# A pause of GpSimd at every twelfth gather of the edge records

## The chip, the cores and the metric

The kernel runs on one core of one Trainium2 chip, as a single launch. The metric is the device time of a run in microseconds (us); several runs are taken, and their median counts. Five engines work side by side, each on its own stream of instructions: TensorE (PE in the profile, its weight loads PEld), VectorE (DVE), ScalarE (ACT), GpSimd (POOL) and SyncE (SP). They meet only through semaphores. 16 DMA engines move data between HBM and SBUF. A gather, which fetches rows named by a list of indices, is issued by GpSimd.

## The reference

Four layers are computed over a graph of 3125 nodes (256 features) and 100000 edges. Each layer adds to `x` a graph part, a mixing part and then a feed-forward part:

```python
edge_index = jnp.stack([src, dst])
xn = _layernorm(x, axis=-1)
x = x + _L0_gnn_ref(xn, ..., src, dst) + _L0_mix_ref(xn[None], ...)[0]
x = x + _L0_ffn_ref(_layernorm(x, axis=-1)[None], ...)[0]
xn = _layernorm(x, axis=-1)
x = x + _L1_gnn_ref(xn, edge_index, edge_type_7, L1_gnn_weights) + _L1_mix_ref(xn[None], ...)[0]
...
```

The graph parts of layers 0, 2 and 3 sum over the edges that end in a node, and need for each edge its source node (`src`), its weight (`edge_weight`) and its attribute (`edge_weight1`). The graph part of layer 1 takes the edges by source and type.

## The kernel before, in words

**Order of the work.** The kernel is a chain of phases. In each phase every engine runs its own part, and a barrier of all engines ends it. First `store_records` writes one record of four numbers per edge (source, weight, attribute, 1) to HBM. `order_by_dst` sorts the edges by the node in which they end. Then `order_by_src` sorts them a second time, by source and type, for layer 1; its sort (`build_sort`) is a bitonic network on VectorE (L239 and L240 are one exchange), with 14 turns in which TensorE transposes the keys in eight pieces (L209) and ScalarE and VectorE take half of the result each (L224, L227, L267, L277). After the transposes of a turn TensorE signals once where the sort has gathers beside it, and twice where it has none.

**The gathers of the change.** Once the order by end node is known, the records have to be brought into it. `fetch_records` does that on GpSimd: 784 gathers, one for each column `k`, each of 128 records of 16 bytes, from `records` in HBM into `dst_order_record` in SBUF. Gather `k` belongs to lane `k % 8`, each lane has a semaphore, and a landed gather adds 16 to it. Before gather `k` is issued, the gather `k - 8` of the same lane must have landed. Nobody needs the records before `unpack_records`, so the gathers are spread in shares over phases in which GpSimd has no other work (`record_share`): 14 beside the making of the second sort's keys, 190 beside that sort, 30 beside `build_run_shares`, 6 beside the order of the chunks, 8 beside the splitting of keys, 18 beside `build_unit_tiles`, 14 beside the loads of `x`, and the other 504 beside the opening of layer 0 (`open0`, by `build_open`).

**The opening of layer 0.** Five groups of five tiles of 125 nodes. For each group VectorE normalizes (L1284 to L1300), TensorE transposes (L1252) and multiplies in pairs of units (L1497) into two pairs of PSUM banks, ScalarE copies each pair out (L1465), five pairs a group. VectorE then does the group's own steps (L1583 to L1603), and TensorE adds the products of keys and values (L1614). The copies go to one buffer `st`, so a group's copies wait until the steps and the products of the group before are done. A group therefore has seven results of TensorE that another engine waits for: the transposes, five pairs, the sum. L1552 is the first instruction of the phase after.

**Other gathers that are named below.** `build_sums` (L602 on GpSimd, L641 on TensorE) makes the two weighted sums of layers 1 and 2, with 880 gathers of 128 rows of 1 KB each; four gathers make a unit. `combine_pairs` (L3197 on GpSimd, L3207 on VectorE) has 50 gathers, and VectorE takes each as it lands.

Of the kernel before, what the change touches and what calls it, by code (L numbers as in the profile page):

```python
# [37 lines left out]
HOTS = 4  # L38
REC = 4
REC_LANES = 8  # L40
SHARES = (14, 190, 30, 6, 8, 18, 14)
EARLY = sum(SHARES)

# [504 lines left out]
def fetch_records(nc, pool, o, first, last):  # L548

    for k in range(first, last):  # L550
        lane, turn = k % REC_LANES, k // REC_LANES
        if turn:
            pool.wait_ge(o["fetched"][lane], 16 * turn)
        nc.gpsimd.indirect_dma_start(o["record"][:, k, :], None, o["records"], bass.IndirectOffsetOnAxis(ap=o["row"][:, k:k + 1], axis=0)  # L554
                                     ).then_inc(o["fetched"][lane], 16)


def record_share(nc, o, n):

    return lambda pool: fetch_records(nc, pool, o, sum(SHARES[:n]), sum(SHARES[:n + 1]))  # L560


def unpack_records(nc, c, o):

    with phase(nc, "unpack", "chain") as s, nc.Block() as block:
        @block.vector
        def _(dve):
            v = nc.vector
            own = Chain(dve, s["chain"])
            for lane in range(REC_LANES):  # L570
                dve.wait_ge(o["fetched"][lane], 16 * (CHUNKS_S // REC_LANES))
            for b in range(TILES - 1):
# [2360 lines left out]
def layer0(nc, c, m, I, dram, by_dst):  # L2933

    with nc.sbuf_tensor("gnn0_to_dst", [R, TILES, D], F32) as to_dst:
        m["to_dst"] = to_dst
        open0(nc, c, m, I, dram, lambda pool: fetch_records(nc, pool, by_dst, EARLY, CHUNKS_S))
        unpack_records(nc, c, by_dst)
        with nc.sbuf_tensor("gnn0_acc", [R, TILES, D + 4], F32) as acc:
            build_attend0(nc, c, by_dst, dram["el0"], to_dst, I["L0_gnn_attn"], acc, dram["pairs"])  # L2940

            def keep(v, own, act_step):

                own(v.tensor_copy(m["deg3"][:], acc[:, :, D + 1:].rearrange("p t k -> p k t")))
            bulk(nc, "degrees", keep)
            close0(nc, c, m, I, acc)
# [352 lines left out]
def build(nc, I, out):  # L3299
# [8 lines left out]
    with ExitStack() as ctx:  # L3308
# [3 lines left out]
        by_dst["record"] = ctx.enter_context(nc.sbuf_tensor("dst_order_record", [P, COLS_S, REC], F32))  # L3312
        by_dst["fetched"] = [nc.alloc_semaphore(f"records_in{l}") for l in range(REC_LANES)]
        by_dst["records"] = dram["records"]
# [37 lines left out]
```

## Time and profile before

| what | value |
|---|---|
| timed runs, median of 3 | 9703.57 us (9694.26 to 9703.69) |
| profiled execution, span from first to last instruction | 10401.4 us |
| profiled execution, time outside the span | none is recorded |
| GpSimd busy in the profiled execution | 4458.2 us (43%) |
| TensorE busy | 6311.5 us (61%) |
| VectorE busy | 4856.6 us (47%) |
| ScalarE busy | 2031.2 us (20%) |

The profile comes from one execution that was recorded by the hardware profiler, and the median from runs that were not recorded. Here the recorded execution is the longer one, by 10401.4 - 9703.6 = 697.8 us. Busy shares are means over stages with different limits, so the stretches and the timeline say more than the shares. In the rows, a time in square brackets is how long the engine had stood idle, and behind the arrow is what ended that idle time; "issue" means that the profile shows nothing that it waited for, and "remote" that the wait was for another engine's signal that can't be tied to one instruction.

### The profile page before, as it was taken

Reading aid. Unit: us, or ns where it says so; the run is one execution under the profiler, and the core shown is the slowest. Engines: PE = TensorE matmul, PEld = TensorE weight load, DVE = VectorE, ACT = ScalarE, POOL = GpSimd, SP = SyncE. Lnnn points to the kernel's source line nnn. Section 1 sums busy time; section 2 is a strip of 40 time slices with the busy share of each in tenths; the row PEclk is TensorE's granted clock in tenths of the full one; section 3 lists DMA queues with packets and bytes.
Section 4 is the critical chain, followed back from the end, with each engine's and each line's share of the span. In section 5 each row is a group of like instructions: output and inputs, shape, how many; then the busy total and the mean of one; then the engine's idle time right before and its main releaser. Section 6 shows DMA issues by size and latency. Waiting matters only on the chain. (4 is left out here: it accounts for less than half of the span.)

```text
span 10401.4 us, 95746 instructions
## 1 busy us (share of the span) xinstructions
PE 6311.5 (61%) x28050; PEld 4795.7 (46%) x28050; DVE 4856.6 (47%) x13537; ACT 2031.2 (20%) x5038; POOL 4458.2 (43%) x4412
## 2 busy tenths in 40 slices
PE   0001115999996865454665444453965788887699
PEld 0000004888884433333443333342863676776466
DVE  7561216888884532222242222264113566666633
ACT  0000002444443210000120000012212232232322
POOL 0546772666660036666104666602020566664000
PEclk9998557999997986666676666675987777777799
DMA  0001002333330133333102333301960232222000
GB/s 12 6 1 28 7 4 71 83 83 83 83 83 14 46 108 92 94 92 92 35 11 70 94 92 92 92 18 25 316 221 27 77 81 80 80 81 64 11 13 19
DMA packets 404431, 697.45 MB, mean 67 GB/s; under 512 B 154143, under 2 KB 267784, under 8 KB 403421
## 3 DMA queue, kind: packets, MB, share of 16 engines
q0 software_dynamic: 206848, 480.68, 17.1%
q1 hardware_dynamic: 197076, 210.68, 6.3%
q8 instruction: 236, 3.87, 0.2%
q14 instruction: 271, 2.22, 0.1%
HBM read 631.46 MB, written 59.47 MB: 66 GB/s over the span
## 5 line engine op out<-in xcount | busy, mean ns | idle before, releaser
L658 POOL DMA_INDIRECT att_rows<-el_table,dst_order_row x1520 | 1589.4, 1046 | 1067.4 <-issue 387.0
L641 PE MATMUL sum_sum<-sum_rows,sum_hot 128*125 128x256 f32 x3520 | 1227.5, 487 | 1291.4 <-issue 817.1
L641 PEld LDWEIGHTS sum_sum<-sum_rows,sum_hot 128*125 128x125 f32 x3520 | 824.8, 240 | 1694.4 <-issue 1540.9
L602 POOL DMA_INDIRECT sum_rows<-rel_table,src_order_row x880 | 833.0, 947 | 1042.3 <-ACTq L593 629.2
L602 POOL DMA_INDIRECT sum_rows<-el_table,dst_order_row x880 | 833.0, 947 | 956.7 <-ACTq L593 543.7
L554 POOL DMA_INDIRECT dst_order_record<-records,dst_order_row x784 | 813.7, 1038 | 589.2 <-PEq L458 297.1
L624 DVE TENSOR_TENSOR gnn_acc<-gnn_acc,sum_sum 125x256 f32 x440 | 180.6, 410 | 1888.8 <-DMA ffn1e_w<-in_L_ffn_W_dram 938.7
L1136 PE MATMUL att_sum<-att_rows,att_hot 128*125 128x265 f32 x1280 | 429.3, 492 | 36.4 <-ACT att_part L1203 30.5
L800 PE MATMUL att_found<-gnn_to_dst,att_hot_t 125*128 x1760 | 437.8, 392 | 2.5 <-ACT att_hot_t L849 1.8
L658 POOL DMA_INDIRECT dst_order_record<-el_table,dst_order_row x240 | 266.1, 1109 | 400.4 <-SPq L960 240.5
L824 PE MATMUL att_sum<-att_rows,att_hot 128*125 128x261 f32 x1760 | 427.3, 385 | 2.4 <-ACT att_rows L862 2.4
L862 ACT ACTIVATE att_rows<-att_rows,att_p 128x257 f32<-128x257 f32 x880 | 375.8, 498 | 0.0
L1101 PEld LDWEIGHTS att_found<-layer_a_dst,att_hot_t 125*128 125x128 f32 x1760 | 275.9, 227 | 180.6 <-issue 159.4
L1136 PEld LDWEIGHTS att_sum<-att_rows,att_hot 128*125 128x125 f32 x1280 | 293.4, 241 | 114.7 <-issue 46.9
L1101 PE MATMUL att_found<-layer_a_dst,att_hot_t 125*128 x1760 | 254.4, 268 | 140.1 <-issue 84.2
L800 PEld LDWEIGHTS att_found<-gnn_to_dst,att_hot_t 125*128 125x128 f32 x1760 | 319.7, 192 | 38.0 <-issue 3.1
L824 PEld LDWEIGHTS att_sum<-att_rows,att_hot 128*125 128x125 f32 x1760 | 314.2, 188 | 47.8 <-ACT att_rows L862 2.5
L744 DVE CUSTOM_DVE_ANT_0 att_high<-att_high,att_att 128x256 f32<-128x256 f32 x880 | 320.0, 418 | 0.0
L1162 ACT COPY att_hot_t<-att_turn_p 125x512 f32<-125x512 f32 x220 | 129.1, 587 | 802.7 <-PE att_turn_p L1091 461.7
L809 PE MATMUL att_spread_p<-ident,att_score 128*125 128x128 f32 x1760 | 251.6, 286 | 43.2 <-issue 27.2
L739 DVE TENSOR_TENSOR att_high<-att_rows,att_found 128x1024 f32<-128x1024 f32 x220 | 268.7, 1222 | 6.5 <-issue 6.5
L809 PEld LDWEIGHTS att_spread_p<-ident,att_score 128*125 128x125 f32 x1760 | 210.0, 188 | 130.6 <-issue 85.1
(775 smaller groups left out, 12593.2 us busy)
## 6 DMA issues: line engine op xcount, KB each, us to landing
block_w<-in_L_ffn_W_dram SPq DMA_DIRECT2D x112, 512.0 KB, 6.3
block_w<-in_L_ffn_W_dram SPq DMA_DIRECT2D x56, 1024.0 KB
att_rows<-el_table,dst_order_row POOLq DMA_INDIRECT x1520
rel_table<-open_st SPq DMA_DIRECT2D x25, 784.0 KB
sum_rows<-rel_table,src_order_row POOLq DMA_INDIRECT x880
sum_rows<-el_table,dst_order_row POOLq DMA_INDIRECT x880
dst_order_record<-records,dst_order_row POOLq DMA_INDIRECT x784
pairs<-zeros SPq DMA_DIRECT2D x1, 7168.0 KB
```

The lines of the kernel that those rows point to most:

```text
L554: nc.gpsimd.indirect_dma_start(o["record"][:, k, :], None, o["records"], bass.IndirectOffsetOnAxis(ap=o["row"][:, k:k + 1], axis=0)).then_ ...
L602: nc.gpsimd.indirect_dma_start(rows[l][:, g, :], None, table, bass.IndirectOffsetOnAxis(ap=o["row"][:, k:k + 1], axis=0)).then_inc(s[f"row ...
L641: last = nc.tensor.matmul(slot(u), hot[u % HOTS_S][:, g, :], rows[l][:, g, :], start=(g == 0), stop=(g == G - 1))
L658: nc.gpsimd.indirect_dma_start(rows[l][:, g, 0:width], None, table, bass.IndirectOffsetOnAxis(ap=o["row"][:, k:k + 1], axis=0)).then_inc(s ...
L739: v.tensor_tensor(high[:], rows[u % LANES_A][:, :, 0:D], found[:], ALU.max).then_inc(s["picked"], 1)
L744: last = v.tensor_tensor_reduce(high[:, g, :], high[:, g, :], att[:], 0.8, 0.0, ALU.mult, ALU.add, score[u % 2][:, g:g + 1])
L800: last = t.matmul(found[:, g, :], hot_t[u % TURNED][:, g * P:(g + 1) * P], nodes_of_unit(to_dst, tile), start=True, stop=True)
L809: last = t.matmul(spread_p[:, g * P:(g + 1) * P], score[u % 2][:, g:g + 1].to_broadcast([P, R]), c["ident"][:], start=True, stop=True)
L824: last = t.matmul(sums[u % 2][:, 0:S], hot[u % HOTS][:, g, :], rows[u % LANES_A][:, g, :], start=(g == 0), stop=(g == G - 1))
L862: last = a.activation(own_rows[:, g, 0:D + 1], own_rows[:, g, 0:D + 1], ACT.Copy, scale=p[u % 2][:, g:g + 1])
L1101: done = t.matmul(found[u % 2][:, g, 0:H], hot_t[u % 2][:, g * P:(g + 1) * P], nodes_of_unit(to_dst, tile), start=True, stop=True)
L1136: done = t.matmul(sums[u % SUMS_B][:, 0:W + 1], hot[u % HOTS_B][:, g, :], rows[u % LANES_B][:, g, :], start=(g == 0), stop=(g == G - 1))
```

## The change

Ahead of a gather whose number within its share is 12, 24, 36 and so on, GpSimd waits until the gather that it issued last has landed. The number of gathers, their order, their lanes and their shares stay as they are.

```diff
@@ -38,6 +38,7 @@
 HOTS = 4
 REC = 4
 REC_LANES = 8
+REST_R = 12
 SHARES = (14, 190, 30, 6, 8, 18, 14)
 EARLY = sum(SHARES)
 
@@ -551,6 +552,8 @@
         lane, turn = k % REC_LANES, k // REC_LANES
         if turn:
             pool.wait_ge(o["fetched"][lane], 16 * turn)
+        if k > first and (k - first) % REST_R == 0:
+            pool.wait_ge(o["fetched"][(k - 1) % REC_LANES], 16 * ((k - 1) // REC_LANES + 1))
         nc.gpsimd.indirect_dma_start(o["record"][:, k, :], None, o["records"], bass.IndirectOffsetOnAxis(ap=o["row"][:, k:k + 1], axis=0)
                                      ).then_inc(o["fetched"][lane], 16)
```

## Rows read from the trace of the kernel before

**Rows 1.** The page: span, and the gathers' group (busy us, mean ns, idle before).

```profile
span 10401.4 us, 95746 instructions
...
L554 POOL DMA_INDIRECT dst_order_record<-records,dst_order_row x784 | 813.7, 1038 | 589.2 <-PEq L458 297.1
```

**Rows 2.** Busy time by stretch: both sorts, the opening with and without gathers.

```profile
44.00:292.00 248.00, 27.57 (x112) 21.97 (x112) 212.72 (x338) 10.02 (x22) 0.00 (x0) 1.00 0.00 0
355.00:706.00 351.00, 27.57 (x112) 21.97 (x112) 213.22 (x338) 8.74 (x21) 191.86 (x190) 1.00 0.03 1
...
914.00:1543.00 629.00, 111.90 (x250) 57.52 (x250) 120.37 (x139) 35.41 (x38) 486.33 (x466) 0.59 0.06 5
1543.00:1676.00 133.00, 43.05 (x108) 23.06 (x108) 65.61 (x37) 10.56 (x12) 0.00 (x0) 0.63 0.04 10
```

**Rows 3.** Timeline of GpSimd: ends of the first share, of the sort's, of the opening's.

```profile
351.35 0.94 POOL L554 DMA_INDIRECT dst_order_record<-records,dst_order_row  x1 [0.30 <-issue]
355.54 1.39 POOL L554 DMA_INDIRECT dst_order_record<-records,dst_order_row  x1 [3.24 <-SPq L202]
...
604.05 0.94 POOL L554 DMA_INDIRECT dst_order_record<-records,dst_order_row  x1 [0.30 <-issue]
...
1541.88 0.94 POOL L554 DMA_INDIRECT dst_order_record<-records,dst_order_row  x1 [0.30 <-issue]
```

**Rows 4.** Timelines of GpSimd, TensorE and VectorE where gathered rows are waited for.

```profile
3763.59 0.95 POOL L602 DMA_INDIRECT sum_rows<-rel_table,src_order_row  x1 [0.30 <-issue]
...
3766.46 3.75 PE L641 MATMUL sum_sum<-sum_rows,sum_hot 128*125 128x256 f32 x8 [0.55 <-DMA sum_rows<-rel_table,src_order_row]
...
7802.18 1.20 POOL L3197 DMA_INDIRECT combine_rows<-results,ffn_place  x1 [0.30 <-DVE X L3207]
...
7806.32 0.48 DVE L3207 SCALAR_TENSOR_TENSOR X<-combine_rows,ffn_gates,X 125x256 f32<-125x256 f32 x1 [0.90 <-DMA combine_rows<-results,ffn_place]
```

**Rows 5.** Timelines of TensorE and ScalarE in the opening, under the gathers.

```profile
985.14 3.55 PE L1497 MATMUL open_unit<-open_w_el,open_xT 128*125 128x512 f32 x4 [16.18 <-ACT open_st L1465]
988.53 1.88 PE L1497 MATMUL open_unit<-open_w_kv,open_xT 128*125 128x512 f32 x4
...
984.08 1.01 ACT L1465 COPY open_st<-open_unit 125x1024 f32<-125x1024 f32 x1 [21.39 <-remote]
1006.48 1.01 ACT L1465 COPY open_st<-open_unit 125x1024 f32<-125x1024 f32 x1 [21.39 <-remote]
1028.88 1.01 ACT L1465 COPY open_st<-open_unit 125x1024 f32<-125x1024 f32 x1 [21.39 <-remote]
```

**Rows 6.** Timeline of VectorE in the opening: starts of a group's work, the stage's end.

```profile
1030.02 1.49 DVE L1583 TENSOR_TENSOR open_row<-open_st,open_bias 125x1280 f32<-125x1280 f32 x1 [104.04 <-ACT open_st L1465]
...
1235.97 1.49 DVE L1583 TENSOR_TENSOR open_row<-open_st,open_bias 125x1280 f32<-125x1280 f32 x1 [139.24 <-issue]
...
1578.60 1.49 DVE L1583 TENSOR_TENSOR open_row<-open_st,open_bias 125x1280 f32<-125x1280 f32 x1 [67.15 <-ACT open_st L1465]
...
1635.22 1.49 DVE L1583 TENSOR_TENSOR open_row<-open_st,open_bias 125x1280 f32<-125x1280 f32 x1 [23.03 <-ACT open_st L1465]
...
1675.71 0.61 DVE L1552 SCALAR_TENSOR_TENSOR KV<-open_kv_p,block 128x128 f32<-128x128 f32 x2 [6.91 <-PEq L86]
```

**Rows 7.** The two sorts by tile: first and last start of the exchanges' first line.

```profile
L239 DVE TENSOR_TENSOR dst_order_keys<-dst_order_keys x153: 691/692/694, 44.9 to 290.4; 128x512 f32<-128x512 f32 x153
...
L239 DVE TENSOR_TENSOR src_order_keys<-src_order_keys x153: 691/692/746, 355.4 to 704.3; 128x512 f32<-128x512 f32 x153
```

**Rows 8.** Timelines of GpSimd and VectorE where the short shares end.

```profile
750.49 1.65 POOL L554 DMA_INDIRECT dst_order_record<-records,dst_order_row  x1 [0.30 <-issue]
...
752.05 6.55 DVE L395 RECIPROCAL src_order_keys<-runs_new 128x1024 f32<-128x1024 f32 x1
...
354.95 0.43 DVE L251 TENSOR_SCALAR src_order_keys<-src_order_keys 128x512 f32<-128x512 f32 x1 [6.19 <-PEq L86]
```

**Rows 9.** The gathers of the two weighted sums: first and last start.

```profile
L602 POOL DMA_INDIRECT sum_rows<-rel_table,src_order_row x880: 940/946/1027, 3754.8 to 4999.8; - x176
```

## The prediction, made before the change was run

> **What bounds the kernel now.** I read the page first, for the gathers' own group, and there the reader is to see that `fetch_records` is a stream of 784 instructions on GpSimd of 1038 ns each, with a small gap between them [rows 1]. Then I cut the busy time by stretch, to see in which stages that stream is the longest thing. In the opening of layer 0 GpSimd works from 914 to 1543 us through 466 gathers, while VectorE has 120 us of work and TensorE 112; in the 133 us that follow there are no gathers at all and the stage still runs [rows 2]. The third look is the timeline of that stage. TensorE ends a pair of units at 988.53 + 1.88 = 990.4 us, and ScalarE copies a pair at 1006.48 and the next at 1028.88, always 22.40 us after the one before [rows 5]. A group of five tiles takes 1235.97 - 1030.02 = 206 us under the gathers and 1635.22 - 1578.60 = 56.6 us once they are over [rows 6]. So something under the gathers delays what TensorE hands on. The two sorts say the same: identical work spans 290.4 - 44.9 = 245.5 us without gathers and 704.3 - 355.4 = 348.9 with 190 of them, 103.4 us more [rows 7].
>
> **Whether those delays are in the timed runs** is what this prediction hangs on. The profiled span is 10401.4 us [rows 1], the timed median 9703.6: 697.8 us of the span are not there without the recording. What would the delays add up to if they were all of the recording's making? 103 in the sort [rows 7]; 133 in the opening, whose work of five groups at 56.6 us (283) fits inside the gathers' 629 [rows 2, 6]; and in the two weighted sums, whose 880 gathers start over 4999.8 - 3754.8 = 1245 us [rows 9] where 879 steps of 0.95 + 0.30 [rows 4] need 1099, 146 each. Together 103 + 133 + 292 = 528 of the 698. No other 500 us that recording could have added is visible to me, so I take it as likelier than not that in the timed runs handed-on results are prompt, and GpSimd's stream alone sets the end of both stages. The Trainium skill, "NOTIFIC — the notification-queue block", section 7.1, says that the block's internal pipeline always holds its producers back rather than lose a record; by that rule the delays belong to the recording. Its section 10 says that a record costs an engine nothing at the rates it measured, which speaks against. No trace of this kind can show the unrecorded run.
>
> **The change part by part.** Nothing is removed or moved. One wait is added ahead of gather k when k - first is 12, 24, ...: in shares of 14, 190, 30, 6, 8, 18, 14 and the last of 784 - 280 = 504 that is 1, 15, 2, 0, 0, 1, 1 and 41, in all 61. It wants all 16 counts of gather k - 1, so it cannot pass before those rows have landed. Queued behind it on GpSimd are only the share's other gathers; who waits for these is the barrier that ends each phase, and last `unpack_records`. The eight-lane wait already there passes more easily after a pause.
>
> *Price of one wait.* No gather of this line is waited for at once in the trace, so I bound it. The fourth gather of a unit in the sums ends at 3763.59 + 0.95 = 3764.54 and TensorE, released by it, starts at 3766.46: 1.92 us. The last gather of the combination ends at 7802.18 + 1.20 = 7803.38 and VectorE takes it at 7806.32: 2.94 [rows 4]; both engines stood idle before, so it was the landing that they waited for. From these the usual gap of 0.30 comes off: 1.62 to 2.64 us. Nothing below 1.62 is likely: these are the quickest landings, and the wait cannot end earlier than the landing. The sums' gathers have the same duration (0.94 to 0.95) as the records' [rows 3, 4], so I stay near that row, but the first gather after a pause took 1.39 instead of 0.94 [rows 3]; I take 1.9. The Trainium skill, "DMA: Bandwidth & Descriptors", section on the anatomy of a DMA of the GpSimd path, gives about 2.0 us fixed for a whole DMA, plus bytes by rate. Counted from the instruction's start that would leave 2.0 - 0.94 - 0.30 = 0.8 us for a wait, an estimate, and by it the sum below would be 46 us and not 109; the landings in the trace (2.87 us from start) disagree, and I go by them.
>
> *The opening, 41 waits.* GpSimd ends at 1542.8 and in the prompt case all else has 629 - 283 = 346 us of room. Nothing hides the waits: 41 x 1.9 = 77.9 us. (If VectorE's work were as long as the stream, they would cost nothing.)
>
> *The sort, 15 waits.* The share runs from 355.54 to 604.99 [rows 3]; the prompt sort, begun at 354.95 [rows 8], would end some 245.5 + 1.4 later, at 602. GpSimd is level with it already, so 15 x 1.9 = 28.5 us. If the stream without recording runs at 1.25 us a gather, it ends at 593 and 9 us of that are covered.
>
> *The short shares.* The first share's last gather ends at 352.29 and the sort's first instruction comes at 354.95 [rows 3, 8]: GpSimd is last there, 1.9 us. In the runs' share the gathers end at 752.14 and VectorE's reciprocal only at 758.60 [rows 8]: 2 x 1.9 = 3.8 are hidden by 6.5 (without that cover, 3.8). The unit tiles' share I cost at nothing, as VectorE's copies close that phase; the one beside the loads of x at half, 1.
>
> Sum: 77.9 + 28.5 + 1.9 + 1.0 = 109.3 us. Within the profiled execution this is added to a prompt version of the span, since its own span contains the disputed 528; against the median, 9703.6 + 109.3 = 9813. With the low price 41 x 1.62 + 15 x 1.62 - 9 = 82, so 9785; with the high one 58 x 2.64 = 153, so 9857.
>
> **The rivals.**
>
> *A, faster: the delays are real and a pause lets everything waiting pass.* For it: while GpSimd stands still nothing is delayed (the last group, 56.6 us). A cycle becomes 12 x 1.25 + 1.9 = 16.9 us. Two pairs of units would pass in one pause, so a group has some five delayed hand-offs instead of seven: 5 x 16.9 + 36 of VectorE's work = 120 us. The opening's work, 5.4 groups (629/206 + 133/56.6), then needs 650 us and fits inside the stream; the stage ends with it at 1621 + 3 instead of 1676, -52. The sort's 103 us of delay would fall to some 68 (eight waits of half a cycle), -35. With 3 us of the short shares: -84, 9620. Against it: the 698 us need another source, and a pause of 2 us is short beside delays of 22. It decides if the opening loses more than 78 of its 133 trailing microseconds.
>
> *B, no change: the delays are real and each pause lets one result pass.* The 22.4 us become 16.9: a group takes 206 - 7 x 5.5 = 167.5 us, by 1621 us 4.2 of 5.4 groups are done and 1.2 x 56.6 = 67 us trail: +12. The sort gains 16, the short shares cost 3. About 9703.
>
> *C, slower by less: the delays are real and the pauses do not touch them.* The stream ends 78 us later, in which 78/206 of a group is done that would have taken 21 us afterwards: +57. The sort, where half of the 28.5 us are under work that goes on anyway, +12; short shares +3. About 9775.
>
> *D, the change does nothing:* if landings came before the next gather is dispatched, every wait would pass at once. The 1.92 us after the instruction's end speak against it; I count it in B.
>
> **How the numbers follow.** My forecast (prompt hand-offs, GpSimd sets the end, 61 waits) has 0.67; A 0.13; B with D 0.13; C 0.07. A measurement tells about 0.2%, 19 us. Slower: forecast and C, 0.74; within 0.2%: 0.13; faster: 0.13. The forecast's own range is 9785 to 9857. To leave out no more than 2 in 10 the range must take in C and B and may leave out A and the outer tails: 9680 to 9862.
>
> **What would show it.** In the changed kernel the gathers' line must wait for its own DMA 61 times more than the 5 of before, near 2.2 us each, 0.3 of it taken from the gaps called issue. The timeline must show such a pause after every twelfth gather and nowhere else. If the recording makes the delays, the span need not grow by 109: it may even shrink where pauses relieve the recording, while the timed median grows; span and median going apart would be the strongest sign for my reading. The step of ScalarE's copies in the opening tells A (several at once), B (about 17 us) and C (22.4). The prediction is wrong if the timed runs have the delays too, or if VectorE's part of the sort is longer than GpSimd's when nothing is recorded, which takes off up to 28.

## The result, and the profile after

| kernel | median, us | runs | span of the profiled run |
|---|---|---|---|
| before | 9698.9 (9688.7 to 9703.7) | 4 | 10401.4 in the first profile, 9692.3 in the second |
| changed | 9814.8 (9811.6 to 9820.4) | 4 | 9810.3 |

The ratio is 1.0125, with a 95% interval from 1.0111 to 1.0140: 116 us slower. Forecast were 9813 and a range from 9680 to 9862.

One thing of the section on the profile before has to be put right here. The recorded execution of the changed kernel is itself one of its four timed runs (9812.4 us, span 9810.3), and so it is in every experiment below; the three first timed runs of the kernel before have no span on record, but all 44 later ones have, 2.1 to 2.2 us under their times. So the later profiles show timed runs, and "recorded" and "timed" are no longer two kinds of execution.

The gathers' line of the changed kernel, by source. It answers to the group in [rows 1]; the list under it says what ended GpSimd's idle time before these gathers, in us, and how often:

```profile
L557 POOL DMA_INDIRECT dst_order_record<-records,dst_order_row x784: 938/944/4736, 334.5 to 1580.4; - x196
...
  issue: 219.8, 715
  DMA dst_order_record<-records,dst_order_row: 162.3, 62
...
DMA to landing us min/median/max: 2.2/2.3/13.8
```

The waits for the own DMA are there: 62 of them, 162.3 us. 61 are the added ones and one is a lane wait, where before has 4 or 5 of these: the pauses have let the others land. The last line gives the time from issue to landing, 2.3 us in the median. The timeline of GpSimd in the opening shows one of the pauses: 2.06 us of idle where 0.30 stands otherwise, twelve gathers after it the next.

```profile
925.82 0.94 POOL L557 DMA_INDIRECT dst_order_record<-records,dst_order_row  x1 [0.30 <-issue]
928.83 0.94 POOL L557 DMA_INDIRECT dst_order_record<-records,dst_order_row  x1 [2.06 <-DMA dst_order_record<-records,dst_order_row]
930.08 0.94 POOL L557 DMA_INDIRECT dst_order_record<-records,dst_order_row  x1 [0.30 <-issue]
...
942.55 0.94 POOL L557 DMA_INDIRECT dst_order_record<-records,dst_order_row  x1 [0.30 <-issue]
945.59 1.92 POOL L557 DMA_INDIRECT dst_order_record<-records,dst_order_row  x1 [2.10 <-DMA dst_order_record<-records,dst_order_row]
```

The span needs care. The profile of the changed kernel is 591 us shorter than the first one of before, while its timed runs are 116 us longer. ScalarE's copies in the opening, which stood 22.40 us apart in [rows 5], are now 3.4 us apart, though the gathers run beside them as before:

```profile
928.78 1.01 ACT L1468 COPY open_st<-open_unit 125x1024 f32<-125x1024 f32 x1 [2.12 <-PE open_unit L1500]
932.13 1.01 ACT L1468 COPY open_st<-open_unit 125x1024 f32<-125x1024 f32 x1 [2.34 <-PE open_unit L1500]
935.57 1.01 ACT L1468 COPY open_st<-open_unit 125x1024 f32<-125x1024 f32 x1 [2.42 <-PE open_unit L1500]
```

So the first profile can't be what the changed kernel is compared with. The first experiment was to take it again.

### The profile page after: what moved, and what is told of

Read it like the earlier page. It is cut to its first block and busy times, and to the rows that moved or that the text cites. A ratio compares the mean times of both kernels' runs of the same rounds, so it can differ in the third digit from the quotient of the medians.

```text
span 9810.3 us, 95807 instructions
## 1 busy us (share of the span) xinstructions
PE 6260.3 (64%) x28050; PEld 4792.7 (49%) x28050; DVE 4858.7 (50%) x13537; ACT 2039.4 (21%) x5038; POOL 4480.7 (46%) x4412
## 5 line engine op out<-in xcount | busy, mean ns | idle before, releaser
L644 PE MATMUL sum_sum<-sum_rows,sum_hot 128*125 128x256 f32 x3520 | 1262.5, 521 | 961.7 <-DMA sum_rows<-rel_table,src_order_row 467.9
L644 PEld LDWEIGHTS sum_sum<-sum_rows,sum_hot 128*125 128x125 f32 x3520 | 863.7, 257 | 1360.5 <-issue 1020.9
L793 PE MATMUL att_turn_p<-ident,att_hot 128*125 128x128 f32 x880 | 155.1, 299 | 468.6 <-DVE att_hot L671 457.6
L793 PEld LDWEIGHTS att_turn_p<-ident,att_hot 128*125 128x125 f32 x880 | 113.5, 188 | 510.4 <-DVE att_hot L671 510.2
L3200 POOL DMA_INDIRECT combine_rows<-results,ffn_place x50 | 61.7, 1233 | 466.6 <-PEq L3194 451.7
```

Of the source, the lines that this page charges most:

```text
L644: last = nc.tensor.matmul(slot(u), hot[u % HOTS_S][:, g, :], rows[l][:, g, :], start=(g == 0), stop=(g == G - 1))
L793: last = t.transpose(turn_p[:, g * P:(g + 1) * P], hot[u % HOTS][:, g, :], c["ident"][:])
```

## The experiments

**The kernel before, profiled again.** No edit.

> The kernel before, unchanged, profiled once more, to see whether the long span of its first profile (10401.4 us beside a median near 9700) belongs to every recording or to that one execution. If every recording delays what TensorE hands on (what my prediction supposed): a span near 10400 again, ScalarE's copies in the opening 22.4 us apart, the second sort 103 us longer than the first. If the delays belonged to that one execution: a span near 9700, copies some 3.4 us apart, the two sorts equally long, and the opening ending with its last gather near 1500. If the delays are in the timed runs too (the rivals), the time itself would have to hold them, and a span near 9700 can't show them.

One run of 9694.4 us, its span 9692.3. The delays are gone: the copies come 3.36 us apart, and the second sort, which spanned 348.9 us in [rows 7], spans 245.9.

```profile
899.54 1.01 ACT L1465 COPY open_st<-open_unit 125x1024 f32<-125x1024 f32 x1 [2.57 <-PE open_unit L1497]
902.90 1.01 ACT L1465 COPY open_st<-open_unit 125x1024 f32<-125x1024 f32 x1 [2.35 <-PE open_unit L1497]
```

```profile
L239 DVE TENSOR_TENSOR src_order_keys<-src_order_keys x153: 691/692/748, 355.5 to 601.4; 128x512 f32<-128x512 f32 x153
...
L602 POOL DMA_INDIRECT sum_rows<-rel_table,src_order_row x880: 942/946/1070, 3541.1 to 4643.7; - x176
```

The gathers of the first sum, from first to last start, take 4643.7 - 3541.1 = 1102.6 us, where they took 1245 in [rows 9]; 879 steps of 1.25 had been reckoned at 1099. All three places that I had added up to 528 us were prompt. And this is a recorded execution, so recording alone doesn't make the delays: they belonged to the one execution of the first profile. Two more executions were recorded to see whether they come back.

> The kernel before, unchanged, a third recorded execution, to see whether the delayed hand-offs of the first profile come back. If they come with a share of the executions: a span near 10400 with some chance. If they were rare: near 9690, as in the second profile.

> The same once more: near 10400 if the delays come often, near 9690 if they are rare.

They ran 9697.2 and 9699.9 us, with spans of 9695.1 and 9697.8. The delays did not come again.

With the second profile of before there is a fair partner. Busy time of each engine in two parts of its opening (us; PE, PEld, DVE, ACT, POOL, granted clock, DMA share, GB/s):

```profile
755.00:1130.00 375.00, 122.14 (x343) 66.49 (x344) 185.84 (x175) 46.76 (x51) 287.39 (x236) 0.76 0.10 15
1130.00:1466.00 336.00, 3.76 (x17) 3.25 (x16) 0.00 (x0) 0.00 (x0) 252.96 (x269) 0.51 0.05 3
```

In the last 336 us GpSimd issues 269 gathers and VectorE and ScalarE do nothing at all: the stage waits for GpSimd alone. In the sort it is the last as well, by some 6 us (the last exchange of VectorE and the last gather of the share):

```profile
601.96 0.68 DVE L240 TENSOR_TENSOR src_order_keys<-src_order_keys 128x512 f32<-128x512 f32 x1
...
607.52 0.94 POOL L554 DMA_INDIRECT dst_order_record<-records,dst_order_row  x1 [0.30 <-issue]
```

Then a ledger of where the 116 us arise, from the places where one phase hands over to the next. Of before, second profile:

```profile
355.03 0.43 DVE L251 TENSOR_SCALAR src_order_keys<-src_order_keys 128x512 f32<-128x512 f32 x1 [6.23 <-PEq L86]
...
616.08 0.98 POOL L330 IOTA runs_place<- 128x1024 int32 x1 [7.62 <-ACTq L327]
...
670.13 0.94 POOL L554 DMA_INDIRECT dst_order_record<-records,dst_order_row  x1 [5.99 <-ACTq L290]
...
732.82 0.94 POOL L554 DMA_INDIRECT dst_order_record<-records,dst_order_row  x1 [13.55 <-PEq L2112]
...
755.06 0.94 POOL L554 DMA_INDIRECT dst_order_record<-records,dst_order_row  x1 [5.08 <-POOLq L86]
...
1463.69 0.94 POOL L554 DMA_INDIRECT dst_order_record<-records,dst_order_row  x1 [0.30 <-issue]
...
1472.05 0.61 DVE L1552 SCALAR_TENSOR_TENSOR KV<-open_kv_p,block 128x128 f32<-128x128 f32 x2 [344.00 <-PEq L86]
```

Of the changed kernel:

```profile
357.02 0.43 DVE L252 TENSOR_SCALAR src_order_keys<-src_order_keys 128x512 f32<-128x512 f32 x1 [7.96 <-PEq L87]
...
644.31 0.98 POOL L331 IOTA runs_place<- 128x1024 int32 x1 [7.62 <-ACTq L328]
...
698.71 0.94 POOL L557 DMA_INDIRECT dst_order_record<-records,dst_order_row  x1 [3.97 <-ACTq L291]
...
761.37 0.94 POOL L557 DMA_INDIRECT dst_order_record<-records,dst_order_row  x1 [11.73 <-PEq L2115]
...
787.08 0.94 POOL L557 DMA_INDIRECT dst_order_record<-records,dst_order_row  x1 [3.45 <-POOLq L87]
...
1580.36 0.94 POOL L557 DMA_INDIRECT dst_order_record<-records,dst_order_row  x1 [0.30 <-issue]
...
1588.71 0.62 DVE L1555 SCALAR_TENSOR_TENSOR KV<-open_kv_p,block 128x128 f32<-128x128 f32 x2 [431.80 <-PEq L87]
```

A share's entry in the last column is how late the changed kernel is where the next phase takes over, less how late it was one line above.

| share | waits | forecast, us | later at its end, us |
|---|---|---|---|
| keys, 14 | 1 | 1.9 | 357.02 - 355.03 = 2.0 |
| sort, 190 | 15 | 28.5 | 28.2 - 2.0 = 26.2 |
| runs, 30 | 2 | 0 | 28.58 - 28.23 = 0.4 |
| chunks, parts, tiles | 1 | 0 | 28.55 - 28.58 = 0.0 |
| loads of x, 14 | 1 | 1.0 | 32.0 - 28.5 = 3.5 |
| opening, 504 | 41 | 77.9 | 116.7 - 32.0 = 84.7 |
| sum | 61 | 109.3 | 116.7 |

Behind the opening both kernels run alike: at its end the changed one is 1588.71 - 1472.05 = 116.7 us late, and at the end of the span 9810.3 - 9692.3 = 118.0.

**The opening's waits alone, and the sort's alone.** In the two kernels the condition reads

```diff
+        if first >= EARLY and k > first and (k - first) % REST_R == 0:
```

and

```diff
+        if first == SHARES[0] and k > first and (k - first) % REST_R == 0:
```

> Only the 41 waits of the opening's share. If GpSimd's stream sets that stage's end: in the profile of the changed kernel a wait stands as 2.06 us of idle instead of 0.30, so 41 x 1.76 = 72 us slower (60 to 90), 0.6 to 0.9%. If all 61 waits cost the same wherever they stand (rival): 41/61 of 116 = 78 us, which this run alone does not tell apart; together with the next run it does. If delayed hand-offs were real in timed runs and pauses relieved them: less than 40 us, or faster.

> Only the 15 waits of the share beside the sort. If GpSimd is level with VectorE there, as I predicted: 15 x 1.76 = 26 us slower, 0.27%. If VectorE's sort is the longer one when nothing is delayed: less, down to nothing. If a pause also makes the rest of the stream slower: more than 26.

The opening's waits: 9790.1 against 9706.6 us, ratio 1.0084 (1.0071 to 1.0098), 82 us. The sort's: 9727.7, ratio 1.0023 (1.0013 to 1.0033), 22 us. 82 + 22 = 104 of 116; the 5.5 us that the ledger gives the first share and the loads of x are in neither, and the other 6 or 7 are within the intervals. The opening has two thirds of the waits and the sort a quarter, so the uniform price of 1.9 us (116/61) would ask for 78 and 29: within their intervals this pair does not refute it. The ledger does, in which three waits beside the runs and tiles cost 0.4 us together. The expectation above had hoped that the two runs together would tell the rival apart; they don't.

**Twice as many waits in the opening.**

```diff
+        if first >= EARLY and k > first and (k - first) % (REST_R // 2) == 0:
```

> Waits in the opening's share alone, but at every sixth gather: 504 / 6 - 1 = 83 instead of 41. If each wait costs its landing less the usual gap (2.07 - 0.30 = 1.77 us) and the stage is GpSimd's throughout: 83 x 1.77 = 147 us, and with the larger price of the first few, which stand under the loads of the weights, up to 165; 1.5 to 1.7%. If the price comes from something that happens once or is bound to the total time (a rival): near the 0.84% of the 41 waits. If pauses let other work pass more quickly: less than twice the 41 waits' price.

9839.2 against 9695.0 us, ratio 1.0149 (1.0134 to 1.0165): 144 us for 83 waits, 1.74 each. 41 cost 82, so the price is paid per wait, and the work of the other engines gains nothing by the pauses. In its trace the waits of the opening read

```profile
POOL dst_order_record L557 <- DMA dst_order_record<-records,dst_order_row: 198.1, 82, 14.5
```

That is more idle time than 144 us ask for, even less the usual gaps (82 x 0.30) and less the 17.1 us of lane waits that before has; another saving hides in the 1.74. The 504 gathers themselves are busy for 521.8 us there, 18.5 less than the 540.4 of the second profile of before. Gathers of 1.8 to 3.5 us, instead of 0.94, are found while VectorE does a group's own steps of up to 2.8 us; before has 35 of them in the opening, this kernel 24. That fewer gathers meet those steps when there are more pauses fits this, but no run was made to show it.

**The same places, but a landing that is already past.**

```diff
+            pool.wait_ge(o["fetched"][(k - 4) % REC_LANES], 16 * ((k - 4) // REC_LANES + 1))
```

> The same 61 places, but the wait is for the gather four back, which was issued some 5 us before and by the landing of 2.2 to 2.3 us from issue has landed. If the price of the change is the landing: same time as before, within 10 us. If it is the wait instruction itself or the break in the stream: slower by tens of microseconds, up to the 116 of the change.

9710.2 against 9706.6 us, ratio 1.0005 (0.9996 to 1.0014): no difference, or at most 14 us, 0.2 a wait. The waiting list of GpSimd in this kernel (us in total, times, longest) shows why:

```profile
POOL dst_order_record L557 <- issue: 222.1, 728, 0.6
POOL dst_order_record L557 <- DMA dst_order_record<-records,dst_order_row: 36.8, 49, 8.4
```

49 idle times are put down to a DMA, but most are the usual gap of 0.3 us, and with the lane waits that before has as well they sum to 36.8 us. Only under the loads had the fourth gather back not landed: the added wait beside the loads of `x` took 3.71 us and one of the first in the opening 4.57. The instruction and the break in the stream cost nothing that can be measured; the landing is the price.

**More results of TensorE under the gathers.** The opening's call loses its pairing:

```diff
-    ... hand=(ACT.Sqrt,), pool_work=pool_work, st_lanes=1, pair=True)
+    ... hand=(ACT.Sqrt,), pool_work=pool_work, st_lanes=1)
```

> The kernel before with the opening's units handed over one by one: ten results of TensorE a group to be copied by ScalarE instead of five pairs, so 25 more hand-offs under the gathers, and no waits added. If hand-offs are prompt in timed runs: they are under GpSimd's stream, which ends some 340 us after the stage's other work, so same time within 10 us. If each result of TensorE needed 22.4 us there, as in the first profile: 25 x 22.4 = 560 us slower, less what follows the last gather.

9696.9 against 9695.0 us, ratio 1.0001 (0.9992 to 1.0010). The edit does add the hand-offs: ScalarE's copies of this kind number 200 instead of 175. With delays of 22.4 us they would have shown, since the stage then trails the gathers ([rows 2]) and nothing covers them. In the timed runs TensorE's results are prompt.

**Eight gathers moved to where GpSimd stood still.**

```diff
-SHARES = (14, 190, 30, 6, 8, 18, 14)
+SHARES = (14, 190, 30, 6, 8, 26, 14)
```

> The kernel before with 8 gathers moved from the opening's share to the one beside the unit tiles (26 instead of 18), no waits added. In the second profile of before GpSimd stands still there for 13.5 us after its last gather. If GpSimd sets the opening's end and is covered beside the tiles: 8 x 1.25 = 10 us faster, 0.1%. If the tiles' phase has no such cover: same.

9683.6 against 9695.0 us, ratio 0.9988 (0.9979 to 0.9997): 11 us faster, and the only kernel of this study that beats both. GpSimd's idle time after the tiles' share fell from 13.55 us (the first gather after it, above at 732.82) to 3.73, and the opening's last gather starts 9.5 us earlier:

```profile
728.53 0.95 POOL L554 DMA_INDIRECT dst_order_record<-records,dst_order_row  x1 [0.30 <-issue]
733.20 0.94 POOL L554 DMA_INDIRECT dst_order_record<-records,dst_order_row  x1 [3.73 <-PEq L2112]
...
1454.23 0.94 POOL L554 DMA_INDIRECT dst_order_record<-records,dst_order_row  x1 [0.30 <-issue]
```

## Why the prediction was right, and where it wasn't

**What bounds the two stages: right.** In timed runs GpSimd's stream sets the end of the opening, with 336 us in which nothing else works, and of the second sort, where it is last too: VectorE's exchanges end at 602.6 us, GpSimd's gathers at 608.5, and the phase after starts with 616.08. The case of a quicker stream, which would have covered 9 us, did not come: 190 gathers took 253 us and not 238. Twice the waits moved the time by their price, and more hand-offs moved nothing.

**Whose the delays were: wrong in its reason, right in its conclusion.** I held that the recording made TensorE's results late, since 528 of 698 surplus microseconds could be added up from them. The sum was near the mark as an account of that execution: against the second profile the same places are longer by 103 us in the sort, 107 in the opening and 142 and 143 in the sums, 495 of 709. But all ten later recorded executions (three of before, one of the changed kernel, six of the experiments) have spans some 2 us under their times, and where the copies were looked at, hand-offs without delay. The Trainium skill, "NOTIFIC — the notification-queue block", section 7.1, on which I had leaned, says that the block's internal pipeline holds its producers back rather than lose a record. None of the ten shows anything of the kind, so recording as such did not make the delays. The one execution can't tell whether that rule was at work in it. What made the results late there stays open: it did not recur in three more executions of the same kernel. The engines did not work more in it (VectorE is busy for 4856.6 us there and 4857.2 in the second profile, TensorE 6311.5 and 6252.3), they waited more. The record doesn't name the chip of the first profile, so a chip of its own is a rival that nothing here excludes. That the conclusion held on a wrong reason is luck in part; what saved the forecast was comparing the span with the median at all. Had I taken [rows 2] and [rows 7] as the timed state, A, B or C would have been the forecast, 9620 to 9775, all too low. The sign that I named, span and median going apart, came, and would have come under either reason: it can't tell a recorder's doing from a rare execution's.

**The price of one wait: 1.9 forecast, 1.76 measured in the plain case** (2.06 - 0.30), near the low bound of 1.62, which the quickest row of the trace gave. The high bound, from `combine_pairs`, was a gather of 1 KB rows with 1.2 us of issue; the records' rows of 16 bytes land 2.3 us after issue. The estimate of 0.8 from the Trainium skill, "DMA: Bandwidth & Descriptors", section on the anatomy of one DMA of the GpSimd path, was too low: 2.3 us from issue stand beside its 2.0, and 46 us beside the 116 measured. The 1.39 us of a first gather after a pause, for which I went above the low bound, were not the rule: at 928.83 it took 0.94, and the 42 of the opening took 1.02 in the mean, no more than the 1.06 of all gathers there.

**The number of waits on the path: right**, 57, and of the one beside the loads of `x` a part, as forecast. The two beside the runs were hidden but for 0.4 us, the one beside the tiles wholly.

**Mis-sized: the waits under other transfers.** I gave the opening 41 equal waits. The first two of them stand while the weights, biases, gains and shifts of the opening are loaded, where a gather lands later. Of the stretch from 785 to 852 us (gathers, and median us from issue to landing):

```profile
dst_order_record<-records,dst_order_row POOLq DMA_INDIRECT x26, 7.8
```

The wait beside the loads of `x` comes just before. In the next rows 781.44 is that one; 819.15 and 849.84 are gathers 12 and 24 of the opening's share, counted from 0. The row of 835.46 is gather 22, which has no added wait: it waits for its lane, as some gathers of the kernel before do.

```profile
781.44 0.94 POOL L557 DMA_INDIRECT dst_order_record<-records,dst_order_row  x1 [5.40 <-DMA dst_order_record<-records,dst_order_row]
...
819.15 0.94 POOL L557 DMA_INDIRECT dst_order_record<-records,dst_order_row  x1 [17.39 <-DMA dst_order_record<-records,dst_order_row]
...
835.46 0.94 POOL L557 DMA_INDIRECT dst_order_record<-records,dst_order_row  x1 [4.14 <-DMA dst_order_record<-records,dst_order_row]
...
849.84 0.94 POOL L557 DMA_INDIRECT dst_order_record<-records,dst_order_row  x1 [12.19 <-DMA dst_order_record<-records,dst_order_row]
```

GpSimd's idle time ahead of the gathers of the opening, of the changed kernel and then of before, second profile (us in total, times, longest):

```profile
POOL dst_order_record L557 <- issue: 142.5, 461, 2.1
POOL dst_order_record L557 <- DMA dst_order_record<-records,dst_order_row: 116.9, 42, 17.4
```

```profile
POOL dst_order_record L554 <- issue: 152.1, 499, 0.3
POOL dst_order_record L554 <- DMA dst_order_record<-records,dst_order_row: 17.1, 4, 9.1
```

The idle time grows by 259.4 - 169.2 = 90.2 us, and the gathers themselves are busy 5.5 us less (534.9 beside 540.4), which gives the 84.7 of the ledger. The last three rows above sum to 33.7 us, where before had its 17.1 us of lane waits; the other 39 waits are plain, (116.9 - 33.7)/39 = 2.13 each. 41 waits at the plain price are 41 x 1.76 = 72.2 us, so the two under the loads make 12.5 us more, net of all this. The wait beside the loads of `x` idled 5.1 us more than the usual gap, of which the end of its phase covered a part: 3.5 us stayed where I had put 1. Together that is 15 us more than my sum, and the lower plain price takes back 57 x 0.14 = 8: 109 + 15 - 8 = 116. So the sum came out near because two errors of size went against each other, and the forecast of 9813 lies nearer to 9814.8 than the 7 us between 109 and 116 because the median of before was 9698.9 in the final comparison, not 9703.6.

**Rivals.** A (faster, pauses let results pass), B and C all needed hand-offs that are late in timed runs. With spans that fit the times in ten of ten later profiles, and the unpaired kernel at 1.0001, none of them holds. Their sums also reckoned with 5.4 groups, where the opening has five (five starts of L1583). D (the waits pass at once) is what the wait for the fourth gather back does, at 1.0005; the change itself does not.

## What to carry to other kernels

Before a profile is taken for the timed run, hold its span against the median: when they differ by more than the change could make, profile again, and reason from the execution whose span fits. A wait for the gather just issued costs the engine its idle time until the landing less the usual gap, 2.06 - 0.30 = 1.8 us here; while the loads of a phase were under way it idled 5 to 17 us. It costs the kernel only where the issuing engine ends last. Where it does, the gain is in moving issues to phases in which that engine stands still.

## What was not expected of the hardware

In one of eleven recorded executions, results of TensorE reached their takers late while GpSimd streamed gathers, in the opening at steps of 22.40 us, and the execution was 7% longer. No other execution of before was: the longest of those on record took 9718.7 us. Three of the later profiles are of the same kernel, so nothing in the kernel makes the difference.

The gathers are also not all alike: in the opening of the second profile 35 of 504 took 1.8 to 3.5 us instead of 0.94, at places where VectorE was at work, so with the lane waits the stream ran at 708.6 / 503 = 1.41 us a gather over the stage, and at 336 / 269 = 1.25 in the part where VectorE stood still.
